# Pipelining a router stage and folding the combine stage and the q, k, v weight splits into the stages beside it

## The reference, cut to what matters

```python
# sublayer 2 of layer 0, on h = gate(x)
logits = einsum('th,eh->te', h, router_w)            # 2048 tokens, 8 experts
top_vals, top_idx = top_k(logits, 2); top_w = softmax(top_vals)
expert, weight = top_idx[:, 0], top_w[:, 0]          # one expert per token
out_e = (silu(h @ gate_w[e].T) * (h @ up_w[e].T)) @ down_w[e].T
x = x + out_e[expert] * weight
# sublayer 1 of layer 1, on h = gate(x): 16 heads of 32, causal softmax attention
qkv = h @ w_attn + b_attn
x = x + attention(q, k, v) @ w_proj + b_proj
```

## Time and profile before

| | |
|---|---|
| time, median of 3 runs | 2551.05 us (2542.93 to 2552.32) |
| the profiled execution: its time, its span | 2549.96 us, 2548.2 us |
| busy in the span: PE, DVE, ACT, POOL | 82%, 70%, 53%, 43% |
| mean granted TensorE clock | 0.914 |
| router block | 1381 to 1501 us |
| experts block | 1501 to 1705 us |
| combine block | 1705 to 1763 us |
| layer-1 attention, until its first projection starts | 1763 to 1789 us |

### The profile page before, as it was taken

The page is one execution under the profiler, slowest core; times in us unless marked ns, Lnnn a source line. Parts: engine busy times, 40 slices in busy tenths (PEclk is TensorE's granted clock), DMA queues, the critical chain, the costliest instruction groups (busy, mean ns, idle before and its releaser), DMA issues. The chain is left out here.

```text
span 2548.2 us, 43637 instructions
## 1 busy us (share of the span) xinstructions
PE 2090.3 (82%) x14585; PEld 1307.8 (51%) x14585; DVE 1778.7 (70%) x3462; ACT 1352.1 (53%) x3201; POOL 1092.8 (43%) x746
## 2 busy tenths in 40 slices
PE   0678888899989999999994549962899898976999
PEld 0355555565555565666662525541566666643444
DVE  7778877888888888887763239855577777653670
ACT  4556565655555555555552413323676767646442
POOL 5656655555555555554441035553232222210440
PEclk9989998999999999999997569985889999988999
DMA  4233223222122121221112664446243333337110
GB/s 162 79 98 93 93 71 105 81 74 70 60 93 82 65 74 60 81 94 57 60 56 103 261 250 138 133 172 251 75 142 101 109 117 103 112 110 250 48 43 23
DMA packets 111809, 270.53 MB, mean 106 GB/s; under 512 B 10416, under 2 KB 40496, under 8 KB 108976
## 3 DMA queue, kind: packets, MB, share of 16 engines
q1 hardware_dynamic: 94128, 219.59, 25.6%
q10 hardware_dynamic: 14976, 40.64, 4.6%
q0 software_dynamic: 2560, 8.39, 0.8%
HBM read 184.70 MB, written 76.55 MB: 103 GB/s over the span
## 5 line engine op out<-in xcount | busy, mean ns | idle before, releaser
L830 PE MATMUL ps_q<-a_y,a_w 128*128 128x512 f16 x1536 | 354.6, 381 | 0.0
L616 POOL TENSOR_TENSOR a_rb<-a_rb,a_rot 128x512 f32<-128x512 f32 x129 | 187.4, 1453 | 307.2 <-ACT a_rb L729 307.2
L830 PEld LDWEIGHTS ps_q<-a_y,a_w 128*128 128x128 f16 x1536 | 149.1, 101 | 162.0 <-issue 2.8
L620 POOL TENSOR_TENSOR a_qk<-a_ra,a_rb 128x512 f32<-128x512 f32 x129 | 203.8, 1580 | 18.9 <-POOL a_rb L616 0.5
L257 DVE TENSOR_TENSOR_SCAN wkv_bwd<-wk_decay,wkv_tail,wkv_fwd 128x512 f32<-128x512 f32 x114 | 199.2, 1769 | 0.1
L880 PE MATMUL ps_g<-a_o,a_wo 128*128 (+1 forms) x768 | 177.8, 381 | 15.0 <-POOL a_o L607 12.5
L839 PEld LDWEIGHTS ps_v<-a_w,a_y 128*128 128x128 f16 x3072 | 176.9, 98 | 15.1
L847 PE MATMUL ps_s<-a_qk 128*128 128x512 f32 (+3 forms) x512 | 173.0, 460 | 13.9 <-POOL a_qk L620 13.9
L839 PE MATMUL ps_v<-a_w,a_y 128*128 128x128 f16 x3072 | 182.0, 219 | 0.0
L869 PE MATMUL ps_o<-a_tt_,a_v 128*128 128x512 f32 (+3 forms) x512 | 173.2, 485 | 9.7 <-ACT a_tt_ L747 8.1
L968 DVE TENSOR_REDUCE a_nmax<-ps_s 128x1 f32<-128x512 f32 (+3 forms) x256 | 124.6, 487 | 73.4 <-PE ps_s L849 66.8
(11 more groups left out here) (263 smaller groups left out, 4943.7 us busy)
## 6 DMA issues: line engine op xcount, KB each, us to landing
a_w<-wqkv_split SPq DMA_DIRECT2D x48, 768.0 KB, 4.3
scratch_numlog<-wkv_nl ACTq DMA_DIRECT2D x40, 512.0 KB, 2.8
wkv_kt<-in_fT ACTq DMA_DIRECT2D x59, 256.0 KB, 2.7
a_wraw<-in_wqkv SPq DMA_DIRECT2D x18, 768.0 KB, 5.4
wqkv_split<-a_w SPq DMA_DIRECT2D x17, 768.0 KB, 6.9
a_stacks<-qk_parts SPq DMA_DIRECT2D x102, 128.0 KB, 2.6
gate_up<-in_gate_up SPq DMA_DIRECT2D x8, 1408.0 KB, 25.8
a_nlc<-scratch_numlog SPq DMA_DIRECT2D x18, 512.0 KB, 4.5
```

Source lines behind the costliest of these rows:

```text
L616: pool.tensor_tensor(rb[:, n, :], rb[:, n, :], rot[:, 2 * n + 1, :], ALU.mult).then_inc(s["roped"], 1)
L620: pool.tensor_tensor(qk[:, n, :], ra[:, n, :], rb[:, n, :], ALU.add).then_inc(s["q_sb"], 1)
L830: mm = pe.matmul(psq[n][:], w16[:, i % 2, wp, n, c, :], y16[:, yp, c, :], start=c + m == 0, stop=c == CC - 1 and m == 2)
```

## The change

**Router.** x1 has two buffers, and the gate is computed in place in them. The gate's inputs are loaded a chunk at a time, each as soon as the chunk before has been used. ACT copies the rows of batch b-1 after it has finished batch b, transposes go to 4 PSUM banks, logits alternate between 2. The maxima are taken per batch, and the 16 additions become one scan. Only 6 experts' weights are loaded here, the last 2 in the expert block.

**Experts.** 6 of the 12 pieces (128 x 512) of the q, k, v weights are loaded and split: one for each of the first 6 pairs of units.

**Combine.** The block is gone. The attention block gathers; 4 tiles are weighed, transposed and added before the gate of batch 0 (into `x3`), 4 between its chunks (into `xm`), and 8 at the ends of heads 0 to 7. Pieces 6 to 11 of q, k, v and the 4 of the projection weights are split in heads 0, 1, 2, 4, 5, 6, 8, 9, 10 and 12. The projections of chunks 2 and 3 wait for their pieces.

The diff, cut to its core:

```diff
-                    if b:
-                        sp.wait_ge(s["sig"], b * CC)
-                    sp.dma_start(xt[:], d["x1"][b].rearrange("c p n -> p c n")).then_inc(s["x_loaded"], 16)
-                    if b:
-                        sp.wait_ge(s["y"], b * CC)
-                    sp.dma_start(nl[:], d["numlog"][1, b].rearrange("c p m n -> p c m n")).then_inc(s["x_loaded"], 16)
-                for e in range(E):
-                    sp.dma_start(w.gate_up[:, e], d["gate_up"][:, e]).then_inc(w.loaded[e], 16)
-                    sp.dma_start(w.down[:, e], d["down"][:, e]).then_inc(w.loaded[e], 16)
+                    if b >= 2:
+                        sp.wait_ge(s["rows_ps"], (b - 1) * TT)
+                    sp.dma_start(xt[:, b % 2], d["x1"][b].rearrange("c p n -> p c n")).then_inc(x_loaded[b % 2], 16)
+                    for c in range(CC):
+                        if b:
+                            sp.wait_ge(s["y"], (b - 1) * CC + c + 1)
+                        sp.dma_start(nl[:, c], d["numlog"][1, b, c]).then_inc(nl_loaded[c], 16)
+                for e in range(EARLY):
+                    w.load(sp, e)
...
+                def take_rows(b):
+                    for t in range(TT):
+                        act.wait_ge(s["rows_ps"], b * TT + t + 1)
+                        act.activation(rows[:, b * TT + t, :], pst[t][:], ACT.Copy).then_inc(s["rows"], 1)
...
-                                       pst[t % 2][:], ACT.Copy).then_inc(s["rows"], 1)
+                        act.activation(y[:, c, :], y[:, c, :], ACT.Exp, scale=-1.0).then_inc(s["inv"], 1)
+                    if b:
+                        take_rows(b - 1)
...
                     mm.then_inc(s["logits_ps"], 1)
                     for t in range(TT):
-                        if t >= 2:
-                            pe.wait_ge(s["rows"], b * TT + t - 1)
+                        if b:
...
+                def take_logits(b):
+                    dve.wait_ge(s["logits_ps"], b + 1)
+                    dve.tensor_copy(logits[:, b * TT:(b + 1) * TT, :],
+                                    psr[b % 2][:, 0:TT * E].rearrange("p (t e) -> p t e", t=TT)).then_inc(s["logits"], 1)
+                    dve.wait_ge(s["logits"], b + 1)
+                    for i in range(b * TT, (b + 1) * TT):
+                        m = dve.max(top[:, i, :], logits[:, i, :])
+                    return m
+
...
-                for i in range(NT):
-                    then(dve.tensor_tensor(before[:, i + 1, :], before[:, i, :], onehot[:, i, :], ALU.add))
+                then(dve.tensor_tensor_scan(upto.rearrange("p e t -> p (e t)"), going[:].rearrange("p e t -> p (e t)"),
+                                            chosen.rearrange("p e t -> p (e t)"), 0.0, ALU.mult, ALU.add))
...
+                for e in range(EARLY):
+                    ready(e)
                 wkv.pool_ekv(pool, 0, 0)
+                for e in range(EARLY, E):
+                    ready(e)
...
                     wkv.join(pool, u, u % 2, u // 2)
+                    if u % 2 and u // 2 < EARLY_PIECES:
+                        w1.pool_low(pool, raw, u // 2)
...
                     if step == 1 and u + 2 < UNITS:
                         wkv.act_load(act, u % 2, (u + 2) // CC, (u + 2) % CC, u + 1)
+                    if step == 1 and u % 2 == 0 and 0 < u // 2 < EARLY_PIECES:
+                        w1.act_load(act, raw, u // 2)
+                    if step == 1 and u % 2 and u // 2 < EARLY_PIECES:
+                        w1.act_split(act, raw, u // 2)
...
+    def act_load(self, act, raw, p):
+        if p:
+            act.wait_ge(self.s["wlo"], p)
+        act.dma_start(raw[:], self.k.d["wqkv1"][p // self.KINDS][:, p % self.KINDS]).then_inc(self.s["raw"], 16)
+
+    def act_split(self, act, raw, p):
+        act.wait_ge(self.s["raw"], p * 16 + 16)
+        act.activation(raw[:], raw[:], ACT.Copy, scale=WSCALE).then_inc(self.s["w64"], 1)
+        act.wait_ge(self.s["w64"], p + 1)
+        act.activation(self.part(p, 0), raw[:], ACT.Copy).then_inc(self.s["whi"], 1)
+
+    def pool_low(self, pool, raw, p):
+        pool.wait_ge(self.s["whi"], p + 1)
+        pool.tensor_tensor(self.part(p, 1), raw[:], self.part(p, 0), ALU.subtract).then_inc(self.s["wlo"], 1)
...
+                def keep(b):
+                    sp.wait_ge(s["x2"], b * TT + TT)
+                    sp.dma_start(d["x2"][b].rearrange("c p n -> p c n"), (xm if b else x3)[:]).then_inc(s["x2_stored"], 16)
+
+                def take_x1(b):
+                    if b >= 2:
+                        sp.wait_ge(s["x2_stored"], b * 16)
+                    sp.dma_start(xm[:], d["x1"][b].rearrange("c p n -> p c n")).then_inc(s["x1_here"], 16)
+
...
-                sp.dma_start(x3[:], d["x2"][0].rearrange("c p n -> p c n")).then_inc(s["first_x"], 16)
+                sp.dma_start(x3[:], d["x1"][0].rearrange("c p n -> p c n")).then_inc(s["x1_first"], 16)
+                take_x1(1)
                 sp.dma_start(nl0[:], d["numlog"][2, 0].rearrange("c p m n -> p c m n")).then_inc(s["first_nl"], 16)
                 sp.dma_start(bqk[:], d["bqkv1"]).then_inc(s["fixed"], 16)
                 sp.dma_start(bv[:], d["bv1"].partition_broadcast(P)).then_inc(s["fixed"], 16)
                 sp.dma_start(bp[:], d["bp1"]).then_inc(s["fixed"], 16)
+                keep(0)
+                keep(1)
+                sp.wait_ge(s["x2_stored"], 32)
                 xg(1, 0, CC)
-                xg(1, 1, CC + 1)
+                take_x1(2)
                 for kind in range(2):
                     stack(0, 0, kind)
...
+                def gather(i):
+                    if i >= 2 * TT:
+                        pool.wait_ge(s["moved"], i - 2 * TT + 1)
+                    pool.indirect_dma_start(got[:, i % (2 * TT), :], None, d["slot_y"],
+                                            bass.IndirectOffsetOnAxis(ap=k.slot[:, i:i + 1], axis=0)
+                                            ).then_inc(gathered[i // TT], 16)
...
+                for i in range(2 * TT):
+                    gather(i)
                 for n in range(CC):
                     y_low(n, n)
+                    gather(2 * TT + n)
                 pool.wait_ge(s["ylo"], CC)
...
                         qk_low(it + 1, 0)
+                        if first:
+                            low_piece(pieces(q)[0])
+                        if first and q == 0:
+                            for i in range(3 * TT, 4 * TT):
+                                gather(i)
                         if q % 2 == 0:
...
+                            late = first and q == 0
+                            if first and i and i - 1 < len(pieces(q)):
+                                load_piece(pieces(q)[i - 1] + 1)
                             if i == 1 and (q or not first):
                                 ot_high(it - 1, (q - 1) % CC)
                             turned_high(h, i)
                             exps(h + 1, i + 1)
                             if i == 0:
...
+                            if i == 3 and late:
+                                y_high(AHEAD % CC, AHEAD)
+                            if first and i < len(pieces(q)):
+                                split_piece(pieces(q)[i])
                             if i == 3 and q % 2:
...
+                def move(i):
+                    pe.wait_ge(s["weighted"], i + 1)
+                    if i >= 2 * TT:
+                        pe.wait_ge(s["o"], i - 2 * TT)
+                    elif i >= 2:
+                        pe.wait_ge(s["x2"], i - 1)
+                    for c in range(CC):
+                        mm = pe.transpose(bank_of(i)[:, c * P:(c + 1) * P], got[:, i % (2 * TT), c * P:(c + 1) * P], k.ident[:])
+                    mm.then_inc(s["moved"], 1)
+
...
+                        pe.wait_ge(w.s["wlo"], n * w.KINDS + kind + 1)
                     for c in range(CC):
+                        if isinstance(n, int) and n + kind == 0:
+                            pe.wait_ge(s["ylo"], c + 1)
                         for m, (yp, wpart) in enumerate(PARTS):
...
+                        pe.wait_ge(s["x2"], 2 * TT + h + 1)
                     for j in range(TT):
...
+                            if first and h < 2 * TT:
+                                move(2 * TT + h)
...
+                def weigh(i):
+                    dve.wait_ge(gathered[i // TT], 16 * TT)
+                    dve.tensor_scalar(got[:, i % (2 * TT), :], got[:, i % (2 * TT), :], k.weight[:, i:i + 1], None,
+                                      ALU.mult).then_inc(s["weighted"], 1)
+
+                def add_moved(i):
+                    dve.wait_ge(s["moved"], i + 1)
+                    if i % TT == 0:
+                        if i < TT:
+                            dve.wait_ge(s["x1_first"], 16)
+                        else:
+                            dve.wait_ge(s["x1_here"], 16 * (i // TT))
+                    x = x2_tile(i)
```

(70 more changed lines are left out.)

294 lines of the change are left out of this document (133 added, 161 removed).

## The result

The changed kernel takes 2531.05 us (median of 6 runs, 2525.72 to 2535.05); measured beside it the kernel before took 2551.41 (2542.93 to 2560.2). The ratio is 0.9922, with a 95% interval of 0.9899 to 0.9946: 20 us faster, where 50 were forecast, and 2531 lies outside the range of 2480 to 2525. The profiled execution took 2525.72 us, with a span of 2524.0. In the rows ACT is ScalarE, DVE is VectorE, POOL is GpSimd and SP is SyncE.

The account below looks back on a forecast made before the run. PE was taken as busy nearly everywhere, with holes in the router and before the first projection. 27 + 43 - 1 - 19 = 50 us gained gave 2500 profiled, 2501 for the median; range 2480 to 2525.

Parts of the forecast that it names:

- Router: Router stage: batches pipeline, with smaller gains in start and tail; 27 us gained, bounds 20 and 36.
- Rival 1: Router: PE gets its full clock in batches 1 to 3; 2493 us, or 2487 if heads hide more; chance 0.2.
- Experts: Experts stage: six weight pieces fit beside PE, which bounds it; 1 us lost, bounds 0 and 6.
- Combine and start of attention: Last expert to q projection: 44.6 us against 88.4; 43 us gained, bounds 36 and 50.
- 18 us for the biases: Start of attention: VectorE first waits 18 us for biases queued behind 4.2 MB, beside 8 gathers.
- Heads 0 to 11: Attention heads: moved tiles, weight pieces and late x1 of batch 3 together cost 19 us, bounds 3 and 45.
- 10 us for 8 tiles: Heads: weighing, transposing and adding 8 tiles costs 2.2 us a head, 17.6 fully exposed, 0 hidden; 10 taken.
- The term for the pieces: Heads: 10 weight pieces at 2.3 us each, mostly inside ACT's wait for transposes; 5 us taken, bounds 0 and 23.
- The term for x1 of batch 3: Heads, tile 12: x1 needs the buffer that batch 2's x2 leaves; 4 us late, bounds 0 and 12.7.
- The rule on the VectorE port: Heads: VectorE and GpSimd block each other on a shared SBUF port; at most 9 us more, expected 2 to 3.
- Rival 4: Heads 0 to 7: DVE and PE wait for each other, each move costing a 6.7 us head; 2568 us, chance 0.03.
- Rival 2: Heads hide little of the moved work: 40 us lost in place of 19; 2522 us, chance 0.14.

Follow-up runs that it names:

- two pairs of runs: Tiles weighed one head ahead, against the changed kernel: 2511.2 us; the same against the changed kernel with a second raw-piece buffer (2518.35): 2499.02 us.
- the other waits mended: Changed kernel with tiles weighed a head ahead, a second raw-piece buffer and the biases' wait behind the gate of four chunks: 2489.13 us.
- the weighing ahead: Changed kernel, but VectorE weighs the tile of head h+1 at the end of its list for head h: 2511.2 us, ratio 0.984.
- all four mendings: Changed kernel with weighing ahead, second raw-piece buffer, biases' wait behind the gate, and x2 stored and x1 loaded tile by tile: 2481.77 us.

## Why the prediction was wrong

- **Router, 27 forecast: right.** 29.0 us by the trace; by itself it makes the kernel 26 to 29 us faster. The groups came within 2.1 us of where they were put, and the reason for the spacing (batch 2's x waits for batch 0's transposes) shows as PE's 8.31 us wait before the third: SyncE issued that load at 1404.22, when PE had ended batch 0's transposes at 1404.19.
- **Rival 1, the full clock: half true and worth nothing.** The second batch's logits took 4.00 us instead of 6.97, so PE did get its full clock there (0.91 granted from 1404 to 1408); but batch 2's x, asked for at 1404.22, landed no earlier for it, and after PE's wait the third and fourth took 6.99 and 6.83 again, at 0.50.
- **Experts, 1 forecast: 2.2,** within the bounds.
- **Combine and start of attention, 43 forecast (88.4 less 44.6 is 43.8): right, 42.4,** by a partly wrong path. 18 us for the biases were 20.7 and the later chunks came faster than the 4.7 us each. I took that wait as a price that the transfers set; the tiles were there after 11.3 us, and 9 us lay in the order of two waits. From the read-out to head 1's scores it was 17.6 us instead of 14.0, within the bound of +5: the parts of q and k landed 7.0 us after their issue.
- **Heads 0 to 11, 19 forecast: 46.1 by the windows, 44.8 up to the first output addition. This is the step that failed,** at or just beyond the end of its bounds of 3 to 45 (the bounds of its three terms by themselves add up to 0 and 53). Its largest term, 10 us for 8 tiles, half of 17.6 exposed, counted durations (0.47, 0.6, 0.68 and two handovers) and asked whether they fit into VectorE's 13.2 us of idle time. As far as that goes it was not too low: eight tiles at the right place cost 4 to 9 us. What it left out is where the weighing stands: not at the end of VectorE's work but at the end of its waits, with PE, in order, held behind it. The place alone cost 20 us (19.9 and 19.3 in two pairs of runs). Part of that is the wait and part the lower clock after it: with the waits filled, PE's own work took 10.5 us less.
- **The term for the pieces, 5: 12.7,** inside its bounds of 0 and 23, but for another reason than work on ScalarE. The prediction knew that the next load waits for GpSimd; it did not look that this wait stands first in ScalarE's list. Most of it (8.3) fell in heads 8 to 11, where no tile waits beside it.
- **The term for x1 of batch 3, 4:** in the changed kernel VectorE stands 2.3 us for it, and PE no more than 0.2 us behind any addition. Only with the other waits mended does it come out in full: 4.7 us on VectorE, and taking it away gained 7.4 us by the medians, 5.1 of them in heads 0 to 7.
- **The rule on the VectorE port: right, and as small as taken.** Three of the eight weighings in the heads took 1.31 to 1.38 us instead of 0.48, each begun beside a subtraction of GpSimd that was already running, 2.6 us together. Three others, begun up to 0.2 us ahead of a GpSimd instruction, took 0.46 to 0.48. One of the three slowed ones, in head 2:

```profile
1768.10 1.34 POOL L1749 TENSOR_TENSOR a_v<-a_vf,a_v 128x512 f16<-128x512 f32 x1 [6.49 <-ACT a_v L1857]
```

```profile
1768.41 1.31 DVE L2207 TENSOR_SCALAR a_got<-a_got,weight 128x512 f32<-128x512 f32 x1
```

  The Trainium skill's Advanced Engine Details and Errata (VectorE Performance Modes) gives the cause; the trace agrees.
- **The rivals.** Rival 4 (slower) came nearest to the mechanism, PE and VectorE each waiting for the other at the end of its list, at a price of a whole head; it cost 4.7 us a head, pieces included. But it put PE's wait behind the addition, and there it measured 0.2 us: the 24.0 us stood one step earlier, at the transposes, for the weighing. The wait for the addition came out only with the weighing ahead, at 5.2 us. Rival 2 had nearly the right sum, 40, and no mechanism of its own. I split between them what was mainly one cause with a price between. Heads 0 to 7 took 89.5 us, half a microsecond short of the 90 that the prediction had named as its refutation.

## What to carry to other kernels

When work is moved into a loop of several engines, ask of each piece not how long it takes but behind which waits it is queued, and which in-order engine must pass it; an operation whose inputs are ready belongs ahead of the next wait, if need be one iteration early. A gain that vanishes may be two separate waits: here one gave 20 us and the other 12, each at the cost of a line or a buffer, and the changed kernel with all four mendings takes 2482 us. And a wait of the matrix engine should be priced above its length wherever the granted clock in its rows falls with it.

## What the runs showed of the hardware

- With 19.4 us of matmuls added to PE's waits the kernel was 11 us faster (6.5 in the stretch itself): PE's granted clock there went from 0.71 to 0.89, and its own work took 54.6 us instead of 65.05. The Trainium skill's TensorE: Matmul & The Clock Gate (What's actually happening) says that the clock follows how busy PE is; the trace agrees. Mending the waits did better than filling them: 0.95 without any useless work.
- The ten transposes of a head's scores took 1.26 us at a granted clock of 1.00 before PE's 5.88 us wait, and 2.01 at 0.62 behind it; at 0.50 throughout (1740.75) they took 2.34.
- With the wait for the biases behind the first four tiles, the last 2 KB of the biases, behind 4.2 MB of loads of x and the gate on their queue, released VectorE 21.9 us after the start of the stage, and the first gathered tiles, issued on another queue, after 11.3.
